# Wide attention in a fused decoder kernel: Q and K projected transposed, scores from 32-row pieces

## The reference, cut to what matters

```python
xn = _layernorm(x)                                   # (128, 64, 128)
q, k, v = xn @ Wq, xn @ Wk, xn @ Wv                  # 16 heads of 64
q, k = rope(q), rope(k)                              # pairs (2i, 2i+1) rotated by position * freq[i]
s = q @ k.T / 8, masked where key > query            # per head 64 x 64
x = x + softmax(s) @ v @ Wo + bo
```

## Time and profile before

| | us |
|---|---|
| median of three runs | 2212.42 (2212.34 to 2218.19) |
| the profiled execution | 2209.22 |
| its span | 2207.2 |
| busy: TensorE, VectorE, GpSimd, ScalarE | 1858, 1557, 1316, 1125 |

### The profile page before, as it was taken

How to read it: one execution, slowest core, us unless ns; L and a number is a source line. 1 busy time by engine, 2 the same in 40 slices (tenths; PEclk the granted TensorE clock), 3 DMA queues, 4 the chain that set the end, 5 groups by cost and what they waited for, 6 DMA issues and landing times. The chain is left out here.

```text
span 2207.2 us, 63464 instructions
## 1 busy us (share of the span) xinstructions
PE 1858.3 (84%) x24029; PEld 1389.7 (63%) x24029; DVE 1557.0 (71%) x3269; ACT 1125.3 (51%) x2119; POOL 1316.0 (60%) x1041
## 2 busy tenths in 40 slices
PE   5999997999984542899999999999999569837776
PEld 3777775777764232466666666666666559626665
DVE  6888885777779652687777777777776777674444
ACT  3677774777753350354454554545544442334444
POOL 3676764777763024576676777766766236207887
PEclk9999997999999766899999999999999879969999
DMA  8000000000003204000000000000000141322221
GB/s 231 15 1 0 0 0 14 17 16 14 15 5 96 76 16 85 15 2 2 1 0 0 0 0 0 0 0 0 0 0 1 48 134 48 98 65 62 66 66 51
DMA packets 102034, 69.66 MB, mean 32 GB/s; under 512 B 12222, under 2 KB 95296, under 8 KB 101552
## 3 DMA queue, kind: packets, MB, share of 16 engines
q1 hardware_dynamic: 89840, 51.72, 8.2%
q0 software_dynamic: 8496, 15.61, 2.8%
q10 hardware_dynamic: 3600, 1.01, 0.2%
HBM read 45.24 MB, written 23.53 MB: 31 GB/s over the span
## 5 line engine op out<-in xcount | busy, mean ns | idle before, releaser
L1260 POOL TENSOR_TENSOR wa_rot<-wa_rot,wa_cross 128x1024 f32<-128x1024 f32 x128 | 302.4, 2362 | 161.7 <-DVE wa_cross L1452 161.7
L1449 DVE TENSOR_TENSOR wa_rot<-wa_ps_qk,cos 128x1024 f32<-128x1024 f32 x128 | 156.1, 1219 | 97.8 <-PE wa_ps_qk L1303 97.5
L1265 POOL TENSOR_TENSOR wa_sd<-wa_sd,wa_mx 128x1024 f32<-128x1024 f32 x64 | 121.7, 1902 | 110.2 <-DVE wa_mx L1469 110.2
L1422 ACT COPY wa_pt<-wa_ps_t 128x1024 f32<-128x1024 f32 x64 | 64.8, 1012 | 235.5 <-PE wa_ps_t L1346 235.5
L324 POOL TENSOR_TENSOR sa_sd<-sa_sd,sa_mx 128x1024 f32<-128x1024 f32 x64 | 121.7, 1902 | 94.0 <-DVE sa_mx L504 93.9
L1323 PEld LDWEIGHTS wa_ps_t<-ident,wa_rot 128*128 128x128 f32 x1024 | 114.7, 141 | 87.1 <-issue 84.1
L324 POOL TENSOR_TENSOR ca_sd<-ca_sd,ca_mx 128x1024 f32<-128x1024 f32 x64 | 121.7, 1902 | 72.5 <-DVE ca_mx L504 72.5
L1323 PE MATMUL wa_ps_t<-ident,wa_rot 128*128 128x128 f32 x1024 | 136.4, 276 | 1.5 <-ACT wa_qt L1400 1.5
L1370 PE MATMUL wa_ps_o<-l_wo,wa_ot 128*128 128x128 f32 x1024 | 127.6, 279 | 8.1 <-ACT wa_ot L1428 8.1
L1303 PE MATMUL wa_ps_qk<-l_wq,wa_xt 128*128 128x512 f32 x256 | 128.5, 625 | 2.2 <-ACT wa_xt L1394 0.4
L1303 PE MATMUL wa_ps_qk<-l_wk,wa_xt 128*128 128x512 f32 x256 | 128.1, 623 | 2.4 <-DVE wa_cross L1452 2.4
(11 more groups left out here) (307 smaller groups left out, 5224.8 us busy)
## 6 DMA issues: line engine op xcount, KB each, us to landing
x_res<-in_x_dram SPq DMA_DIRECT2D x16, 256.0 KB, 7.1
ca_ctx_t<-in_ctx_t_dram SPq DMA_DIRECT2D x64, 64.0 KB, 1.8
x_dram<-xp_row SPq DMA_DIRECT2D x16, 256.0 KB, 2.3
xn_dram<-r_xn SPq DMA_DIRECT2D x16, 256.0 KB, 2.3
x_res<-x_dram SPq DMA_DIRECT2D x16, 256.0 KB, 5.3
cs_ctx_t<-in_ctx_t_dram SPq DMA_DIRECT2D x16, 256.0 KB, 2.8
l_ffn<-in_f_w_dram SPq DMA_DIRECT2D x2, 2048.0 KB, 11.5
cm_ctx<-in_ctx_dram SPq DMA_DIRECT2D x16, 256.0 KB, 2.9
```

What stands on the lines that cost most here:

```text
L1260: pool.tensor_tensor(rot[n][:], rot[n][:], cross[n][:], ALU.add).then_inc(rotated[n], 1)
L1265: pool.tensor_tensor(sd[:, v], sd[:, v], mx[:, v].unsqueeze(2).to_broadcast([P, H1, SEQ]), ALU.subtract).then_inc(sub_ready, 1)
L1449: dve.tensor_tensor(rot[n][:].rearrange("p h s d -> p (h s) d"), src.rearrange("p h s d -> p (h s) d"), bc(k.cos[:], 1, 2 * H1), ALU.mult)
```

## The change

`project` makes Q and K with channels on the partitions: weight blocks of 128x128 are stationary and `xt` streams, 8 products of 128 columns per projection. The weights are laid out so that a block holds, for four heads, either the first or the second members of the rotation pairs: 4 heads x 32 rows. `rot` has the two halves in separate blocks, so each product of rotation is over whole blocks; cosine and sine now are [128, 128] tables (channel x position). The transposes of Q and K, their copies on ScalarE and the turns for `ps_t` go.

`scores` takes a head's 64 rows as two pieces of 32 that accumulate. Four row groups of the array hold four heads, each with a PSUM bank of its own in `ps_svt` (4 banks), two column halves the two sequences: 128 matmuls of 32 rows and 64 columns. V shares the first two banks with the scores, the transposed P the other two. So the scores now wait also for the copy of P two tiles back, and the P transposes wait until VectorE has taken the scores of the same step. The mask is one addition of a table of NEG instead of two multiply-adds. `rot` is double buffered. V's copy and K's addition on GpSimd move a step later. Heads are reordered in Wv and Wo to match. Shortened:

```diff
-        rot = [sb(f"rot{n}", [P, H1, 2, HALF]) for n in range(2)]
-        cross = [sb(f"cross{n}", [P, H1, 2, HALF]) for n in range(2)]
-        qt = sb("qt", [P, 2, PAIRS, P])
-        kt = sb("kt", [P, 2, PAIRS, P])
+        rot = [sb(f"rot{n}", [P, 2, 2, QUADS, P]) for n in range(2)]
+        cross = [sb(f"cross{n}", [P, 2, QUADS, P]) for n in range(2)]
+        later_keys = sb("later_keys", [P, QUADS, SEQ])
...
-        ps_sv = ps("ps_sv", [P, 2, 512])
-        ps_t = ps("ps_t", [P, PAIRS, P])
+        ps_svt = ps("ps_svt", [P, 4, 512])
         ps_o = ps("ps_o", [P, 2, GROUP, P])
-        scores_ps = ps_sv[:].rearrange("p b (h s) -> p (b h) s", s=SEQ)
+        scores_ps = ps_svt[:, :, 0:QUADS * SEQ]
+        v_ps = ps_svt[:, 0:2].rearrange("p b (n d) -> p b n d", d=D1)
+        pt_ps = ps_svt[:, 2:4].rearrange("p b (n t) -> p (b n) t", t=P)
...
-                for stage, behind in ((divide, 3), (add_bias, 4), (rotate(0), 1), (subtract_max, 2), (rotate(1), 1)):
+                for stage, behind in ((rotate(1), 2), (divide, 3), (add_bias, 4), (rotate(0), 1), (subtract_max, 2)):
...
                     for half in range(2):
-                        mm = pe.matmul(ps_qk[:, half], xt[:, v % 2], weight[:, half * 512:(half + 1) * 512],
-                                       start=True, stop=True)
+                        for j in range(QUADS):
+                            mm = pe.matmul(ps_qk[:, half, j * P:(j + 1) * P], weight[:, half, j], xt[:, v % 2],
+                                           start=True, stop=True)
...
             def scores(i, t, v):
-                pe.wait_ge(qk_t_ready[0], t + 1)
-                pe.wait_ge(qk_t_ready[1], t + 1)
+                pe.wait_ge(rotated[0], t + 1)
                 pe.wait_ge(v_ready, t + 1)
-                pe.sem_inc(scores_begun, 1)
-                for m in range(PAIRS):
+                if late(t, 2):
+                    pe.wait_ge(pt_ready, t - 1)
+                pe.wait_ge(rotated[1], t + 1)
+                for j in range(QUADS):
                     for half in range(2):
-                        of = slice(half * SEQ, (half + 1) * SEQ)
-                        for b in range(2):
-                            rows = slice(b * SEQ, (b + 1) * SEQ)
-                            mm = pe.matmul(scores_ps[rows, half * PAIRS + m], qt[of, v % 2, m, rows],
-                                           kt[of, v % 2, m, rows], start=True, stop=True)
+                        for h in range(4):
+                            of = slice(h * ROWS, (h + 1) * ROWS)
+                            for b in range(2):
+                                rows = slice(b * SEQ, (b + 1) * SEQ)
+                                mm = pe.matmul(scores_ps[rows, h, j * SEQ:(j + 1) * SEQ], rot[0][of, v % 2, half, j, rows],
+                                               rot[1][of, v % 2, half, j, rows], start=(half == 0), stop=(half == 1))
                 mm.then_inc(s_made, 1)
 
             def p_transpose(i, t, v):
                 pe.wait_ge(p_ready, t + 1)
-                wait_for_turn(pe, "p", i)
+                if has(i - 2, NT):
+                    pe.wait_ge(s_taken, i - 1)
...
-                for stage, behind in ((project(0), 1), (qk_transpose(1), 2), (out_project, 4), (x_transpose, 0),
-                                      (scores, 2), (project(1), 1), (p_transpose, 3), (project_v, 1),
-                                      (qk_transpose(0), 1), (values, 3)):
+                for stage, behind in ((project(0), 1), (out_project, 4), (x_transpose, 0), (scores, 2), (project(1), 1),
+                                      (p_transpose, 3), (project_v, 1), (values, 3)):
...
-                for stage, behind in ((o_copy, 4), (normalise, 0), (k_copy, 2), (x_copy, 0), (p_copy, 3),
-                                      (exponential, 2), (v_copy, 1), (q_copy, 1)):
+                for stage, behind in ((o_copy, 4), (v_copy, 2), (normalise, 0), (x_copy, 0), (p_copy, 3), (exponential, 2)):
...
-                for half in range(2):
-                    masked = dve.scalar_tensor_tensor(out=by_half[:, half], in0=bc(k.future[:], 1, PAIRS), scalar=NEG,
-                                                      in1=scores_ps[:, half * PAIRS:(half + 1) * PAIRS],
-                                                      op0=ALU.mult, op1=ALU.add)
-                masked.then_inc(s_taken, 1)
+                dve.tensor_tensor(sd[:, v].rearrange("p (h j) s -> p h (j s)", h=4), scores_ps,
+                                  bc(later_keys[:].rearrange("p j s -> p (j s)"), 1, 4), ALU.add).then_inc(s_taken, 1)
```

More of the change, by code:

```diff
@@ L1182, in wide_head_attention @@
     NT = k.tiles
-    HALF = D1 // 2
+    QUADS = H1 // 4
+    ROWS = D1 // 2
     scale = float(D1) ** -0.5
@@ L1225, in wide_head_attention @@
         rotated = [sem("q_rotated"), sem("k_rotated")]
-        qk_t_made = [sem("qt_made"), sem("kt_made")]
-        qk_t_ready = [sem("qt_ready"), sem("kt_ready")]
+        mask_made = sem("mask_made")
         v_made, v_ready = sem("v_made"), sem("v_ready")
@@ L1232, in wide_head_attention @@
         pt_made, pt_ready = sem("pt_made"), sem("pt_ready")
-        scores_begun, values_begun = sem("scores_begun"), sem("values_begun")
+        values_begun = sem("values_begun")
         ot_made, ot_ready = sem("ot_made"), sem("ot_ready")
@@ L1237, in wide_head_attention @@
         LAST = 4
[L1239 to L1250, removed]
         nc.scalar.preload_act_table(ACT.Exp)
@@ L1259, in stage @@
                     pool.wait_ge(crossed[n], t + 1)
-                    pool.tensor_tensor(rot[n][:], rot[n][:], cross[n][:], ALU.add).then_inc(rotated[n], 1)
+                    pool.tensor_tensor(rot[n][:, v % 2], rot[n][:, v % 2], cross[n][:], ALU.add)\
+                        .then_inc(rotated[n], 1)
                 return stage
@@ L1312, in project_v @@
                     for half in range(2):
-                        mm = pe.matmul(ps_sv[half * SEQ:(half + 1) * SEQ, b], xt[:, v % 2, b * SEQ:(b + 1) * SEQ],
+                        mm = pe.matmul(ps_svt[half * SEQ:(half + 1) * SEQ, b], xt[:, v % 2, b * SEQ:(b + 1) * SEQ],
                                        k.l1_wv[:, half], start=True, stop=True)
                 mm.then_inc(v_made, 1)
[L1317 to L1321, removed]
-                    for m in range(PAIRS):
-                        mm = pe.transpose(ps_t[:, m], flat[:, m], k.ident[:])
-                    mm.then_inc(qk_t_made[n], 1)
-                return stage
             def scores(i, t, v):
-                pe.wait_ge(qk_t_ready[0], t + 1)
-                pe.wait_ge(qk_t_ready[1], t + 1)
+                pe.wait_ge(rotated[0], t + 1)
                 pe.wait_ge(v_ready, t + 1)
-                pe.sem_inc(scores_begun, 1)
-                for m in range(PAIRS):
+                if late(t, 2):
+                    pe.wait_ge(pt_ready, t - 1)
+                pe.wait_ge(rotated[1], t + 1)
+                for j in range(QUADS):
                     for half in range(2):
-                        of = slice(half * SEQ, (half + 1) * SEQ)
-                        for b in range(2):
-                            rows = slice(b * SEQ, (b + 1) * SEQ)
-                            mm = pe.matmul(scores_ps[rows, half * PAIRS + m], qt[of, v % 2, m, rows],
-                                           kt[of, v % 2, m, rows], start=True, stop=True)
+                        for h in range(4):
[4 more added lines that the diff above has]
+                                               rot[1][of, v % 2, half, j, rows], start=(half == 0), stop=(half == 1))
                 mm.then_inc(s_made, 1)
@@ L1342, in p_transpose @@
                 pe.wait_ge(p_ready, t + 1)
-                wait_for_turn(pe, "p", i)
+                if has(i - 2, NT):
+                    pe.wait_ge(s_taken, i - 1)
                 flat = sd[:, v].rearrange("p (n h) s -> p n (h s)", h=2)
                 for m in range(PAIRS):
-                    mm = pe.transpose(ps_t[:, m], flat[:, m], k.ident[:])
+                    mm = pe.transpose(pt_ps[:, m], flat[:, m], k.ident[:])
                 mm.then_inc(pt_made, 1)
@@ L1394, in x_copy @@
                 act.copy(xt[:, v % 2], ps_o[:, 1, 0]).then_inc(xt_ready, 1)
[L1396 to L1406, removed]
             def v_copy(t, v):
@@ L1411, in v_copy @@
                     act.wait_ge(ot_made, t - 3)
-                act.copy(v_sb[:, v], ps_sv[:].rearrange("p b (n d) -> p b n d", d=D1)).then_inc(v_ready, 1)
+                act.copy(v_sb[:, v], v_ps).then_inc(v_ready, 1)
             def exponential(t, v):
@@ L1421, in p_copy @@
                     act.wait_ge(ot_made, t - 1)
-                act.copy(pt[:, v % 2], ps_t[:]).then_inc(pt_ready, 1)
+                act.copy(pt[:, v % 2], pt_ps).then_inc(pt_ready, 1)
             def o_copy(t, v):
@@ L1446, in stage @@
                     if late(t, 1):
[L1447 to L1452, removed]
+                        dve.wait_ge(rotated[n], t)
```

(28 more changed lines are left out.)

3 lines of the change are left out of this document (1 added, 2 removed).

## The result

| | before | after |
|---|---|---|
| median of four runs each, us | 2214.91 | 2245.36 (2242.49 to 2250.26) |
| ratio | | 1.0139 (1.0113 to 1.0164) |
| span of the profiled execution, us | 2207.2 | 2242.4 |
| busy: TensorE, ScalarE | 1858, 1125 | 1812, 1009 |

What follows compares the result with a forecast made beforehand. TensorE was taken to bound the wide attention at 12.55 us per tile; 12.40 after the change gives -10 us over 64 tiles, 12 jumps +21, so 2220, or 2223 on the median's scale; range 2144 to 2290.

Steps and rivals of the forecast that it cites:

- part 1: Wide attention, TensorE: the 16 transposes of Q and K per tile go, saving 1.90 us.
- Part 2: Q and K projections as eight matmuls of 128 columns: 1.79 us each, together -0.06 us per tile.
- Part 3: Scores as 128 matmuls, 256 records, eight pieces at once: 2.04 us, +0.94 per tile; upper bound 3.9 us.
- Part 4: Other engines and new waits: the VectorE round trip of 7.1 us hides within 7.5, so TensorE stays the bound.
- Part 5: Instruction fetch in TensorE's loop: four steps become 3,080 instructions, some 12 packets, taken as not kept in the engine.
- Part 5 (a): Scores: 512 instructions use up two packets, giving one fetch stall of 0.87 us per step (0.1 to 1.6).
- L: Time from asking for an instruction packet to its landing: taken as 1.8 us, between 1.0 and 2.5.
- Part 5 (b): TensorE's loop end: each of 12 jumps back waits 1.8 us for its packet, +21 us (12 to 30).
- The first rival: TensorE's loop: fetching costs nothing, as it is kept or fetched far ahead; -65 us, 2147 us; chance 0.22.
- The second rival: Scores: array or instruction supply (7.3 ns each) allows four pieces at once, 3.9 us; 2266 to 2287 us; chance 0.29.

Runs made afterwards that it cites:

- the first experiment: Changed kernel with TensorE's loop of two unrolled steps in place of four, and two buffers in place of four; 2155.15 us, ratio 0.9649 to the kernel before.
- the moved loop: Changed kernel with a two-step loop and every score matmul issued twice, 14 steps instead of 12 written out ahead of the loop; 2273.7 us, ratio 1.027.
- the shortened loop: Changed kernel, still four steps, with the second 32-row score piece left out for two of the four blocks of heads; 2187.9 us, ratio 0.982.
- the doubled scores: Changed kernel with a two-step loop and every score matmul issued twice, 12 steps written out ahead; 2630.3 us, ratio 1.18.
- the last experiment: Changed kernel with a two-step loop and doubled score matmuls, 14 steps instead of 12 written out ahead of the loop; 2273.7 us, ratio 1.027.

## Why the prediction was right, and where it was off

It said slower, 2223 us, with 2144 to 2290 around it; it came to 2245. The reason was the right one: the longer loop is not kept, and the jumps pay for it. But that the side came out right was partly luck, since two terms were off by much and in opposite directions. With the measured step of 11.22 us and my 21 us for the jumps the sum would have been 64 x -1.33 + 21 = -64 us, and would have said clearly faster.

- *TensorE's list of matmuls sets the stage; part 1.* Right. The transposes' 1.90 us are gone, and no wait has taken their place.
- *Part 2*, Q and K: 1.89 each, not 1.79. +0.14 us per step where -0.06 stood.
- *Part 3, scores.* I counted 128 matmuls, and the description of the change says so too; the loops over j, half, h and b make 4 x 2 x 4 x 2 = 64. All that hangs on it was doubled: 256 records (128), 512 instructions (256), 2.04 us (1.52). The rate was not right either: 64 matmuls eight at once in rounds of 58 ns would be 0.93 + 0.17 = 1.10 us; they take 1.52. Eight pieces at once run at 10.6 ns a record, four quadrants at 14.5, so twice the tiles give 1.4 times the rate, not twice. The assumed rate of eight in 58 ns does hold, but only within the first 32 records of a burst. This fits a queue that is used up and then filled at 5.3 ns an instruction, but no run varied the supply alone. Step: 11.53 forecast without stalls, 11.22 measured.
- *Part 4*, the other engines. Right: VectorE waits 0.55 and 0.70 us for Q's projection before its rotation in two steady steps (expected 0.4 to spare), and no engine holds TensorE there:

```profile
1318.13 1.23 DVE L1419 TENSOR_TENSOR wa_rot<-wa_ps_qk,cos 128x1024 f32<-128x1024 f32 x1 [0.70 <-PE wa_ps_qk L1292]
```

- *Part 5, are the instructions kept.* Right that they are not. The eleven packets of a round look like the 12 of the prediction, but those came from 3,080 instructions; 2,093 touch ten. I also took everything above 6 packets as not kept, where seven are: the first experiment and the moved loop show kept ones, the shortened loop and the eight-step loop of the kernel before others that are not. The size of the Trainium skill ("Runtime: NRT & Kernel Launch", Instruction fetch mechanics), 128 KiB in blocks of 16 KiB, is eight packets; the runs keep loops that touch seven and fetch those that touch eight anew, which agrees if one is the block fetched ahead; the two rounds at eight packets that were kept don't fit that.
- *Part 5 (a)*, a stall of 0.87 us in each step's scores. It isn't there in most steps, because of the count: 256 instructions are one packet. Where the burst was made 512 instructions long, the hole came, with 1.5 to 2.4 us and larger than forecast. The same kind of wait, in a kernel that I had miscounted, and with the L of 1.8 us that also sank (b): the lines of the last experiment make it some 4.
- *Part 5 (b)*, 1.8 us per jump. This is the mis-sized term: 8.5 to 9.9 us. I bounded it by the landing of one packet. What is missing is, first, that the halt itself is 4.8 us, of which over 2 us follow the landing; second, another halt of 1.5 us (and more at the lower clock) since this loop begins close to a packet's end; third, that after the halt TensorE runs at 1.2 GHz for some microseconds, which the change paid 2 to 3 us for.

So 12.40 us per step was 1.18 too much, 76 us over the stage, and 21 us for the jumps were 90 too few; the steps written out cost 8 more that no term had. The sum landed 20 us low. The first rival, fetching for free, was what the change could have been: with jumps to kept instructions it comes to 0.965 of before, 2135 us on its scale, against 2147 given for it. The second rival's supply limit is half there, at 5.3 instead of 7.3 ns.

What stays open: why two rounds of the doubled scores were kept when the others weren't; whether 10.6 ns per record is the supply or the array; and what TensorE waits for in the 2 us between the landing of its packets and its start.

## What to carry to other kernels

Before an unrolled loop's step gets more instructions, count them for the whole body: the gain of 1.33 us per step, 84 us in all, was lost to 12 jumps that cost 111. If instruction packets show up within a loop where there were none, unroll less (two steps instead of four gave 5% here) or write the loop out (the same 5%). Count a nest of loops by multiplying its ranges, before anything is built on the number.

## What the runs showed of the hardware

A jump back to kept instructions cost TensorE 0.2 us, one to instructions that are not kept 5 to 10 us: a halt of 3.3 to 5.3 us, with some loops a second one of 0.9 to 1.5, and matmuls at the 1.2 GHz level behind it. Whether a loop of 1,561 instructions is kept hung on 25 instructions of place: 1.18 against 1.03 of before. In straight code bursts of 256 score instructions went through in most steps and stopped by 0.6 to 1.2 us in some; bursts of 512 stopped by 1.5 to 2.4 us in nearly every step.
